# Norm, transposes, logits and top eight of each row tile moved into the graph blocks; slots taken from ranks first, one-hots split over engines

## The reference

```
x  = x + graph_L(layernorm(x), adj)            # L0: scores from two MLPs; L1, L3: attention; L2: adj by kind
xn = layernorm(x)                              # per row, eps 1e-5
lg = xn @ gate_w (+ gate_b)                    # 16, 8, 8, 16 experts
w, e = top2(softmax(lg))                       # weights renormalised in L0, L2, L3
x  = x + sum_k w_k * ffn_{e_k}(xn)             # L2: plus a shared expert; L0: a second norm
```

## Time and profile before

| | us |
|---|---|
| runs | 1241.56 median of 3 (1239.06 to 1244.21) |
| profiled execution | 1240.28 |
| its span, first to last instruction | 1238.2 |
| PE busy in the span | 981.2 |
| DVE busy | 738.7 |
| ACT busy | 513.4 |
| POOL busy | 456.6 |

### The profile page before, as it was taken

One profiled execution on the slowest core, in us unless ns is written; L12 is line 12 of the kernel. 1 busy time (PEld: TensorE's weight loads), 2 busy tenths in 40 slices (PEclk: granted clock), 3 DMA queues, 4 the chain that ended last, 5 costly groups with the idle time before them and its releaser, 6 DMA issues. The chain is left out here.

```text
span 1238.2 us, 24351 instructions
## 1 busy us (share of the span) xinstructions
PE 981.2 (79%) x7766; PEld 910.4 (74%) x7766; DVE 738.7 (60%) x1715; ACT 513.4 (41%) x943; POOL 456.6 (37%) x572
## 2 busy tenths in 40 slices
PE   5785888437888869748985999999738996699993
PEld 1674877425877759747985999999734885699993
DVE  3666655575788556557334666666454675566664
ACT  2241655300566337513011777777403451244441
POOL 1131554212789227510001455555303440254441
PEclk9697999768899979979986999999958997799997
DMA  6002965400000156632214575553030001547763
GB/s 221 1 2 70 335 225 156 139 12 1 1 1 2 36 175 196 199 112 60 86 35 182 199 290 165 200 187 114 23 127 0 2 1 35 224 167 229 257 211 119
DMA packets 65853, 148.42 MB, mean 120 GB/s; under 512 B 10704, under 2 KB 42736, under 8 KB 59760
## 3 DMA queue, kind: packets, MB, share of 16 engines
q1 hardware_dynamic: 55792, 120.17, 27.9%
q0 software_dynamic: 9984, 27.28, 7.3%
HBM read 203.88 MB, written 18.87 MB: 180 GB/s over the span
## 5 line engine op out<-in xcount | busy, mean ns | idle before, releaser
L1394 PE MATMUL r_pH<-e_xsT,e_w 128*128 128x128 f32 x2624 | 321.4, 281 | 24.5 <-DMA e_w<-w_in 21.9
L1394 PEld LDWEIGHTS r_pH<-e_xsT,e_w 128*128 128x128 f32 x2624 | 309.9, 196 | 29.8 <-issue 16.8
L1342 POOL DMA_INDIRECT y_rows<-e_ys,e_to x104 | 188.9, 1816 | 268.0 <-DVE e_idx L1462 137.0
L1430 ACT ACTIVATE e_w_hi<-e_w 128x1024 fp32r<-128x1024 f32 (+1 forms) x104 | 136.2, 1310 | 118.6 <-DMA e_w<-w_in 117.3
L1407 PE MATMUL r_pY<-e_w_hi,e_h_hi 128*128 128x256 f32 x544 | 164.2, 302 | 9.1 <-issue 4.5
L1474 DVE TENSOR_TENSOR e_w_lo<-e_w,e_w_hi 128x1024 fp32r<-128x1024 f32 (+1 forms) x104 | 160.6, 1544 | 17.5 <-ACT e_w_hi L1430 15.9
L1479 DVE TENSOR_TENSOR e_h_lo<-xnT,e_h_hi 128x512 fp32r<-128x512 f32 (+1 forms) x104 | 88.9, 855 | 129.8 <-ACT e_h_hi L1446 129.6
L1407 PE MATMUL r_pY<-e_w_hi,e_h_lo 128*128 128x256 f32 x544 | 155.5, 286 | 0.0
L1407 PE MATMUL r_pY<-e_w_lo,e_h_hi 128*128 128x256 f32 x544 | 155.3, 286 | 0.0
L352 PE MATMUL g_o<-g_V,g_pT 128*128 128x65 f32 (+2 forms) x896 | 138.7, 309 | 14.8 <-ACT g_pT L312 14.8
L1442 ACT ACTIVATE xnT<-r_pH,e_w 128x128 f32<-128x128 f32 x432 | 119.4, 376 | 73.4 <-PE r_pH L1394 73.3
(11 more groups left out here) (258 smaller groups left out, 1444.0 us busy)
## 6 DMA issues: line engine op xcount, KB each, us to landing
e_w<-w_in SPq DMA_DIRECT2D x60, 1024.0 KB
e_w<-w_in SPq DMA_DIRECT2D x72, 512.0 KB
e_w<-w_in SPq DMA_DIRECT2D x32, 1028.0 KB
e_w<-w_in SPq DMA_DIRECT2D x44, 514.0 KB
e_b<-b_in SPq DMA_DIRECT2D x76, 128.0 KB
e_w<-y_rows SPq DMA_DIRECT2D x24, 256.0 KB, 5.3
p_adj<-adj_in SPq DMA_DIRECT2D x8, 512.0 KB, 7.5
xn_rows<-xn SPq DMA_DIRECT2D x4, 1024.0 KB, 4.4
```

What stands on the lines that cost most here:

```text
L1342: pool.indirect_dma_start(out=y_rows[:, :], in_=ys[b][:, :], in_offset=None, out_offset=bass.IndirectOffsetOnAxis(ap=to[b][:, :], axis=0))\
L1394: ins = nc.tensor.matmul(pH[b % 2][:, f, :], w1[b][:, at:at + P], xsT[b % 2][:, c, :], start=(c == 0), stop=(c == DC - 1))
L1430: nc.scalar.activation(w2_hi[b % 2][:, :], w2[b][:, :], ACT.Copy).then_inc(w2_rounded, 1)
```

## The change

Per row tile, `Front` does the norm, the two transposes, the logits and the top eight. `attend` wraps `attention` and puts these pieces into its steps once a row tile is finished (`done(t)` is the DVE step at which the tile's last unit ends: t+4 in level 0, 4t+7 in level 1, 2t+7 in level 3); `graph2` places them by hand. What doesn't fit into the loop comes after it, inside the same block. SP stores each tile of `xn` as it comes and waits for the stores in the graph block. The gate's norm, transposes, logits, top eight and its 56 `rouse` matmuls are gone. Level 0's addition of the per-row bias goes from the end of the attention to its preparation and into `finish`. In the routing, the position within an expert is taken from the ranks first (`nth`), so that the slot is known before the tiles are; the slot's one-hots are 16 operations on POOL, one of the three columns of numbers is made by ACT; the softmax weights come after `tiles_known`, the scatter table (`dest`) after `rows_known`. POOL no longer waits for `rows_known` and the store before its loop; the gathers still wait for `idx_ready`. SP issues the `b2` load of tile t-2 ahead of tile t's weights instead of behind them.

The diff, cut, its indentation shortened; removed gate lines are those listed above:

```diff
+class Front:
...
+def store(self, sp):
+    for t in range(NT):
+        sp.wait_ge(self.xn_ready, t + 1)
+        sp.dma_start(xn_rows[t * P:(t + 1) * P, :], xn[:, t, 0:D]).then_inc(self.stored, 16)
+    sp.wait_ge(self.stored, 16 * NT)
+def moments(self, dve, t):
+    nc.vector.bn_stats(out=stats[:, t, :], in_=x[:, t, :]).then_inc(self.linked, 1)
+    dve.wait_ge(self.linked, t + 1)
+    nc.vector.bn_aggr(out=mean_var[:, t, :], in_=stats[:, t, :]).then_inc(self.var_ready, 1)
+def invert(self, pool, t):
+    pool.wait_ge(self.var_ready, t + 1)
+    nc.gpsimd.tensor_scalar(mean_var[:, t, 1:2], mean_var[:, t, 1:2], EPS, None, ALU.add)\
+        .then_inc(self.raised, 1)
+    pool.wait_ge(self.raised, t + 1)
+    nc.gpsimd.tensor_tensor(rstd[:, t, :], mean_var[:, t, 1:2], power[:, t, :], ALU.pow)\
+        .then_inc(self.rstd_ready, 1)
+def norm(self, dve, t):
+    dve.wait_ge(self.rstd_ready, t + 1)
+    nc.vector.tensor_scalar(xn[:, t, 0:D], x[:, t, :], mean_var[:, t, 0:1], rstd[:, t, :],
+                            ALU.subtract, ALU.mult).then_inc(self.xn_ready, 1)
+def turn(self, pe, t):
+    n = len(self.tp)
+    pe.wait_ge(self.xn_ready, t + 1)
+    if t >= n:
+        pe.wait_ge(self.xnT_ready, t - n + 1)
+    for c in range(DC):
+        ins = nc.tensor.transpose(self.tp[t % n][:, c, :], xn[:, t, c * P:(c + 1) * P], ident[:, :])
+    ins.then_inc(self.turned, 1)
+def place(self, act, t):
+    act.wait_ge(self.turned, t + 1)
+    nc.scalar.activation(xnT[:, :, t * P:(t + 1) * P], self.tp[t % len(self.tp)], ACT.Copy)\
+        .then_inc(self.xnT_ready, 1)
+def logits(self, pe, t):
+    if t == 0:
+        pe.wait_ge(self.loaded, self.ALL)
+    else:
+        pe.wait_ge(self.ranked, t)
+    pe.wait_ge(self.xnT_ready, t + 1)
+    for c in range(DC):
+        ins = nc.tensor.matmul(self.psl[:, t, :], xnT[:, c, t * P:(t + 1) * P], self.gw[:, c, :],
+                               start=(c == 0), stop=(c == DC - 1))
+    ins.then_inc(self.summed, 1)
+def rank(self, dve, link, t):
+    dve.wait_ge(self.summed, t + 1)
+    if t == 0:
+        dve.wait_ge(self.loaded, self.ALL)
+    if self.gb_name:
+        ins = nc.vector.tensor_tensor(lg[:, t, 0:self.E], self.psl[:, t, :], self.gb[:, :], ALU.add)
+    else:
+        ins = nc.vector.tensor_copy(lg[:, t, 0:self.E], self.psl[:, t, :])
+    ins.then_inc(self.ranked, 1)
+    dve.wait_ge(self.ranked, t + 1)
+    link(nc.vector.max(out=v8[:, t, :], in_=lg[:, t, 0:self.E]))
+    nc.vector.max_index(out=i8[:, t, :], in_max=v8[:, t, :], in_values=lg[:, t, 0:self.E])
...
+def turn_at(t):
+    return max(done(t) + 2, free)
+def place_at(t):
+    return max(done(t) + 3, free + 1)
+def logits_at(t):
+    return max(done(t) + 4, free + 2)
+def rank_at(t):
+    return logits_at(t) + 1
...
+def vector_step(u, dve, link, finished):
+    if "vector_step" in more:
+        more["vector_step"](u, dve, link, finished)
+    for t in range(NT):
+        if done(t) + 1 == u:
+            front.norm(dve, t)
+        if done(t) == u:
+            measure(dve, finished, t)
+        if rank_at(t) == u:
+            front.rank(dve, link, t)
+def vector_end(dve, link, finished):
+    if "vector_end" in more:
+        more["vector_end"](dve, link)
+    for t in range(NT):
+        if done(t) + 1 >= units + 4:
+            if done(t) >= units + 4:
+                measure(dve, finished, t)
+            front.norm(dve, t)
+    for t in range(NT):
+        if rank_at(t) >= units + 4:
+            front.rank(dve, link, t)
+def tensor_step(u, pe, maxed):
+    if free and u == free:
+        pe.wait_ge(maxed, units)
+    for t in range(NT):
+        if logits_at(t) == u:
+            front.logits(pe, t)
+        if turn_at(t) == u:
+            front.turn(pe, t)
+def tensor_end(pe):
+    for t in range(NT + 1):
+        if t < NT and turn_at(t) >= units + 3:
+            front.turn(pe, t)
+        if t > 0 and logits_at(t - 1) >= units + 3:
+            front.logits(pe, t - 1)
...
+def pool_end(pool):
+    for t in range(NT):
+        if done(t) >= units:
+            front.invert(pool, t)
...
+            dve.wait_ge(copied, 4)
+            link(nc.vector.tensor_tensor(f01[:, 1, :], f01[:, 1, :], f01[:, 0, :], ALU.subtract))
+            nc.vector.tensor_tensor(x[:, :, OUT:D], x[:, :, OUT:D], bc(f01[:, 0:1, :], [P, NT, OUT]), ALU.add)
...
+    def finish(u, dve, link, o, gm):
+        nc.vector.tensor_scalar(has[:, u:u + 1], gm, MASKED / 2, None, ALU.is_gt)
         link(nc.vector.reciprocal(r[:, u:u + 1], o[:, OUT:OUT + 1]))
+        link(nc.vector.scalar_tensor_tensor(
+            out=x[:, u, OUT:D], in0=f01[:, 1, :], scalar=has[:, u:u + 1], in1=x[:, u, OUT:D],
+            op0=ALU.mult, op1=ALU.add))
         return nc.vector.scalar_tensor_tensor(
             out=x[:, u, OUT:D], in0=o[:, 0:OUT], scalar=r[:, u:u + 1], in1=x[:, u, OUT:D],
             op0=ALU.mult, op1=ALU.add)
...
+        front.store(sp)
...
+            if t >= 3:
+                front.logits(pe, t - 3)
+            if t >= 2:
+                front.turn(pe, t - 2)
+        for t in range(NT - 2, NT):
+            front.logits(pe, t - 1)
+            front.turn(pe, t)
+        front.logits(pe, NT - 1)
...
+        for t in range(NT):
+            front.invert(pool, t)
...
+        for t in range(NT):
+            front.place(act, t)
...
             nc.vector.tensor_tensor(x[:, t, :], x[:, t, :], pso[t % 2][:, :], ALU.add).then_inc(added, 1)
+            if t >= 1:
+                front.norm(dve, t - 1)
+            dve.wait_ge(added, t + 1)
+            front.moments(dve, t)
+            if t >= 4:
+                front.rank(dve, link, t - 4)
+        front.norm(dve, NT - 1)
+        for t in range(NT - 4, NT):
+            front.rank(dve, link, t)
...
-    rouse(tps[3][:, 0, :], 56)
...
     pe.wait_ge(placed, 1)
+    pe.wait_ge(weighted, 1)
+    pe.wait_ge(on_slots, 1)
     for q in range(2 * NT):
         ins = nc.tensor.matmul(pst[:, :, :], on_slot[:, q, :], token[:, q, :, :],
                                start=(q == 0), stop=(q == 2 * NT - 1))
     ins.then_inc(mm, 1)
-    rouse(tps[3][:, 0, :], 72)
+    rouse(spare, 72)
...
+    act.wait_ge(on_tiles, 1)
+    nc.scalar.activation(token[:, :, 1, :], on_tile[:, :, :], ACT.Copy, scale=iota_p[:, :]).then_inc(weighted, 1)
...
+    pool.wait_ge(slots_known, 1)
+    for q in range(2 * NT):
+        ins = nc.gpsimd.tensor_scalar(on_slot[:, q, :], iota_row[:, :], slot_f[:, q:q + 1], None, ALU.is_equal)
+    ins.then_inc(on_slots, 1)
...
         ins = nc.vector.tensor_tensor(oh[:, k, :, :], bc(iota_row[:, 0:E].unsqueeze(1), [P, NT, E]),
-                                      bc(idx[:, :, k:k + 1], [P, NT, E]), ALU.is_equal)
+                                      bc(i8[:, :, k:k + 1], [P, NT, E]), ALU.is_equal)
     link(ins)
     nc.vector.tensor_tensor(both[:, :, :], oh[:, 0, :, :], oh[:, 1, :, :], ALU.add).then_inc(onehot, 1)
-    nc.vector.tensor_tensor(ez[:, :, :], lg[:, :, :], bc(v8[:, :, 0:1], [P, NT, E]), ALU.subtract)
+    nc.vector.tensor_tensor(ez[:, :, :], lg[:, :, 0:E], bc(v8[:, :, 0:1], [P, NT, E]), ALU.subtract)
     nc.vector.tensor_tensor(den[:, 0, :], v8[:, :, 1], v8[:, :, 0], ALU.subtract).then_inc(centred, 1)
+    if shared:
+        nc.vector.tensor_copy(dest[:, 0:first], own[:, 0:first])
+        nc.vector.memset(etab[0:1, 0:first], E)
+    dve.wait_ge(mm, 1)
+    for k in range(2):
+        ins = nc.vector.tensor_tensor(nth[:, k, :, :], oh[:, k, :, :], psr[:, :, :], ALU.mult)
+    link(ins)
+    link(nc.vector.tensor_reduce(posf[:, :, :], nth[:, :, :, :], AX.X, ALU.add))
+    link(nc.vector.tensor_copy(pos[:, :, :], posf[:, :, :]))
+    pairs = pos[:, :, :].rearrange("p k t -> p (k t)")
...
+    link(nc.vector.tensor_reduce(base[:, :], prev[:, :, :], AX.X, ALU.add))
+    nc.vector.tensor_tensor(upto[:, :], base[:, :], tiles[:, :], ALU.add)
+    for k in range(2):
+        ins = nc.vector.tensor_tensor(start[:, k, :, :], oh[:, k, :, :], bc(base[:, :].unsqueeze(1), [P, NT, E]),
+                                      ALU.mult)
+    link(ins)
+    nc.vector.tensor_scalar(used[:, :], iota_un[:, :], upto[:, E - 1:E], None, ALU.is_lt)
+    link(nc.vector.tensor_reduce(startf[:, :, :], start[:, :, :, :], AX.X, ALU.add))
+    nc.vector.tensor_tensor(tile_f[:, :, 0], startf[:, :, :].rearrange("p k t -> p (k t)"), tile_i[:, :], ALU.add)
+    link(nc.vector.tensor_reduce(turns[:, :], used[:, :], AX.X, ALU.add))
...
+    nc.vector.tensor_tensor(on_tile[:, :, :], bc(part_row[:, 0:R].unsqueeze(1), [P, 2 * NT, R]),
+                            bc(place[:, :, :], [P, 2 * NT, R]), ALU.is_equal).then_inc(on_tiles, 1)
+    dve.wait_ge(on_tiles, 1)
+    for row, n in ((token_row, 0), (side_row, 2)):
+        ins = nc.vector.tensor_tensor(token[:, :, n, :], on_tile[:, :, :],
+                                      bc(row[:, :, :].rearrange("p k t -> p (k t)").unsqueeze(2), [P, 2 * NT, R]),
+                                      ALU.mult)
+    ins.then_inc(placed, 1)
...
```

(23 more changed lines are left out.)

322 lines of the change are left out of this document (149 added, 173 removed).

## The result

The changed kernel takes 1247.21 us in the median of 20 runs, the kernel before on the same chip 1241.3: ratio 1.0061, 95% interval [1.0043, 1.0079]. On another chip it came out at 1.0047 [1.0021, 1.0072]. The prediction was 1222, range 1203 to 1245, a gain of 1.6%: what came is a loss. The profiled execution spans 1245.3 us (before 1238.2), mean clock 0.884 (0.895).

The account below looks back on a forecast made before the run. No engine was taken to be at its limit (PE 79%); the gate's serial fronts and routing lay on the path. Gains of 12.7 (fronts), 6.0 (routing) and 1.0 (bias loads), 19.7 us, gave 1222, range 1203 to 1245.

Parts of the forecast that it names:

- Fronts removed, 67.4 us: Gate's four norm-to-top-eight chains, four index casts and level 0's bias additions leave the path: 67.4 us gained.
- tails 25.5: Front work left behind each graph loop's last unit: 9.7, 4.2, 6.0 and 5.6 us over the levels, 25.5 lost.
- the turn of logits and rank: In the tails, each tile's logits wait for the previous tile's to be read: 0.9 us a tile.
- GpSimd's two operations: In each tail's chain, two one-column operations between moments and norm: 0.7 us for both with the hand-over.
- Level 1's loop: Attention loop of level 1: new pieces partly land on the unit's cycle, 8 us lost, bounds 0 to 16.
- Level 2's loop: graph2's loop: PE full, six tiles' work 3.7 us plus waits of 1.9 for the rank, 5.7: 9.4 us lost.
- The routing, -6.0: From `both` to the first gather or weights: 1.5 us shorter in each of four levels, 6.0 gained.
- the one-hot of 0.35 us: Routing: each of POOL's sixteen slot one-hots takes 0.35 us, 5.6 together; bounds 0.29 to 0.8 each.
- rival 2's second half: Routing: a POOL one-hot takes 0.8 us, 7.2 us a level later, 1251 us; rival's chance 0.12 in all.
- Rival 2's first half: Routing: DVE's ten two-input operations each wait for a POOL one-hot, 14 us worse, 1236; rival's chance 0.12 in all.
- The bias loads: Experts: loading `b2` a tile earlier, ahead of the weights, gains 1 us, bounds -1 to 6.
- rival 3: Loops and tails: the front's pieces are serial and cost their full length, 27 us worse, 1249; chance 0.13.

Follow-up runs that it names:

- g3: All four norms moved, ranks batched at levels 0 and 2, one-hots split, bias order old, throwaway matmuls in level 1's loop: 1215.7 us, 0.9805 to the kernel before.
- f2: The changed kernel with the second bias loaded behind the weight loads again: 1239.8 us, ratio 1.0004 to the kernel before.
- g4: The changed kernel with 24 throwaway matmuls ahead of each of level 2's logits that wait for the rank: 1235.8 us, ratio 0.9959 to the kernel before.
- f3: The changed kernel with level 2's rank of tile t-4 moved ahead of VectorE's wait for the sum: 1235.1 us, ratio 0.9954 to the kernel before.
- f4: The changed kernel with the ranks of all tiles batched behind the loop in all four graph blocks: 1238.3 us, ratio 0.9997 to the kernel before.

## Why the prediction was wrong

- *Fronts removed, 67.4 us, and tails 25.5.* Right in kind, the tails too small. Level 0 and level 3 came out within 1.2 us of the sum. From the end of the last addition to `x` to `both` the tails are 11.6 at level 0 (9.7 in the sum), 6.2 at level 1 (4.2 and the store's 0.8), 9.1 at level 2 (6.0) and 8.2 at level 3 (5.6): 35.1 for 26.3. Cut in the same way, what fell away is 70.5 for 67.4, so 5.7 us are left as too small a price. The term at fault is the turn of logits and rank, 0.9 us in the sum, between its 0.75 at full clock and 1.1 at half: it took 1.3 at clock 0.50, and 2.1 at level 2, where ACT's copy stands in it. GpSimd's two operations took 1.0 with the hand-over and not 0.7. At level 0 the tail's 1.9 too much was made up by chance: 0.7 more fell away, the loop cost 0.5 less and the preparation 0.9 less than priced.
- *Level 1's loop, 8 us, bounds 0 to 16.* This is the first step that failed. It went from 118.1 to 134.5: 16.4. The mechanism that was named, new pieces on the cycle, is there, and its 8 us were about right: where the clock holds the loop grew by 7.4 (g3, its fill included), with one late stretch by 8.2 (f2). The stage takes 131.7 us in g3 and 132.5 in f2 and g4, and the sum had 131.9. The missing term is PE's clock. 20.5 us at half clock at 0.40 are 8.2 us, of the 8.8 by which the stage is off. The prediction read the clock of the fronts and let it act only in the tails; it did not ask whether an engine with 10 to 15% of slack keeps its clock when its gaps are moved together.
- *Level 2's loop, 9.4 us.* Measured 10.7 from the first addition to the last. Six tiles' work and three waits were right; a wait costs 3.8 us where the clock falls, not 1.9. The tail was 3 us short. The wait is also a cost that one moved call removes, worth 0.9% (f3).
- *The routing, -6.0.* Measured +4.6 by the stages. The failed step is one number, the one-hot of 0.35 us. It takes 0.60 alone and 0.69 on the average at level 3. Sixteen take 11.05 us at levels 0 and 3 and 10.1 at levels 1 and 2, and not 5.6 + 2 = 7.6. At level 3 they are done 14.2 us after `both` and not 10.7, which is 3.5 of the 3.8 us by which the gather is later than priced (17.4 for 13.6). The parts that the prediction names add up to 12.9; no part explains the other 0.7 of its 13.6. The range held 0.8, the choice went to the nearest row (a 128 x 128 select at 0.288), which is another operation. The row scaled from [128 x 8], in rival 2's second half, gave 0.8 and was nearer.
- *Rival 2's first half, GpSimd holds DVE*, did not occur. The Trainium skill, "SBUF — State Buffer", section "SBUF: two separate sides", has the port pair as a lock that blocks the other side whichever comes first. The trace agrees for one direction: POOL's operations are longer beside DVE's in the earlier trace rows and after (a one-hot 1.31 for 0.60). It does not for the other: DVE's two-input operation of 128x512 (L1302) takes 0.691 us before and 0.693 after, where it starts in the midst of the one-hots, with 0.03 us idle ahead of it in both. The measurement decides: here only POOL pays.
- *The bias loads, +1, bounds -1 to 6.* Lost 5 us (1.0047 to 1.0004, and 1.0038 alone), outside the bounds. The wait that was looked at was the one removed, 28.0 us on DVE; the one that was moved, SyncE's for a finished tile, went ahead of the weight loads (12.5 us in 16 times for 3.2 in one), and that queue's order was not priced. That the 5 us come by this wait is likely and not shown.
- *The rivals.* The time fell near rival 3 (1249), by luck, since it came another way: it asked for 27 us in loops and tails alone, from pieces that cost their full length. What came is 13.5 from loops, tails and their clock, 10.6 from the routing and, by the timed runs, about 5 from the bias loads.

In the profiled pair the experts show +1.6 for those 5; that stage goes from 703.7 to 720.9 us over the 17 profiles, so there the timed runs are the better witness. Open stays what sets the number of half-clock stretches at level 1 (one to three late ones in kernels with the same loop; six in f4, whose loop has less VectorE work), and why the routing alone was not slower in its timed runs.

The best version, g3, with all four norms moved, ranks batched at levels 0 and 2, the rank of level 2 out of PE's way (there by batching), eleven one-hots on GpSimd, the old place of the bias loads and PE kept busy at level 1, takes 1215.7 us, ratio 0.9805. That is 0.4% under the predicted 0.984. So most of the change is worth having once its costs are taken out one by one.

## What to carry to other kernels

Work that fits into an engine's slack can still cost TensorE its clock: look at where the idle gaps will lie after the change, and price a gap both ways, at its length and, if the clock falls behind it, at about twice that (1.7 us of waiting cost 3.2). An operation without a row is priced by its own kind or by both ends of its range, since here one number, 0.35 for 0.60 us, turned a gain of 6 us into a loss. A queue's wait is priced with what stands behind it: taking 28 us of waiting from VectorE gained nothing, and an order that put SyncE's 12.5 us of waiting ahead of the weight loads cost 5.

## What the runs showed of the hardware

- TensorE at level 1 fell to half clock for 7 us (ten in a few cases) behind two waits of 0.71 and 1.12 us with 1.09 us of work between, and behind waits of 0.61, 0.77 and 0.85 us in one place but not in the next. The loop of before, with waits of about 0.5 us a unit (11.9 us in 24 times from 330 us on, the longest 0.85), kept 1.00. With matmuls of ones in the gaps (g3) it stayed at 1.00, although they add some 15 us of work.
- GpSimd's compare of 128x128 with a column takes 0.60 us, 1.0 to 1.31 beside VectorE's operations of 128x512; its operations on one column take 0.18 to 0.29 and up to 1.28 beside VectorE, and the power on one column 0.56 to 1.48. VectorE's operations of 128x512 and 128x256 in the routing kept their times beside the one-hots (0.691 and 0.693, 0.424 and 0.424 us).
